# Moving the next batch's convolution on TensorE from the start of a slot to the end of the one before, with VectorE's order kept

## What is computed

```python
h = layernorm(x) * (1 + ca) + sa
xz = h @ in_proj_w.T;  x_, z = split(xz)             # 256 + 256 channels
u  = silu(causal_conv4(x_) + conv_b)                 # depthwise, 4 taps
dt, Bm, Cm = split(u @ x_proj_w.T)                   # 8 + 16 + 16
delta = softplus(dt @ dt_w.T + dt_b)
state_t = state_{t-1} * exp(delta_t * A) + (delta_t * u_t) * B_t   # 256 x 16 states
y_t = sum_n state_t[n] * C_t[n]
x = x + ga * ((y + u * D) * silu(z)) @ out_proj_w.T
h = layernorm(x) * (1 + cb) + sb
x = x + gb * (shared_ffn(h) + top2_of_8_expert_ffn(h))             # exact gelu, 256 hidden
```

## Time and profile before

| | |
|---|---|
| median of 3 runs | 685.6 us (685.33 to 688.16) |
| the profiled execution | 684.8 us |
| its span in the profile | 683.1 us |
| PE busy | 593.3 us (87%) |
| DVE busy | 598.3 us (88%) |
| ACT busy | 489.7 us (72%) |
| POOL busy | 320.2 us (47%) |
| mean granted TensorE clock | 0.955 |

### The profile page before, as it was taken

How to read it: one execution, slowest core, us unless ns; L and a number is a source line. 1 busy time by engine, 2 the same in 40 slices (tenths; PEclk the granted TensorE clock), 3 DMA queues, 4 the chain that set the end, 5 groups by cost and what they waited for, 6 DMA issues and landing times.

```text
span 683.1 us, 9767 instructions
## 1 busy us (share of the span) xinstructions
PE 593.3 (87%) x3646; PEld 466.5 (68%) x3646; DVE 598.3 (88%) x713; ACT 489.7 (72%) x861; POOL 320.2 (47%) x171
## 2 busy tenths in 40 slices
PE   5684478899989998999989998999979947998897
PEld 4243345689657965788567966787668936798686
DVE  5399999999999999999999999999998999798416
ACT  3689535999589976989589957998598925962460
POOL 1036556446654556446653656446543664464000
PEclk9787589999999999999999999999999968999999
DMA  7423333314432235133531343223522442220000
GB/s 221 161 92 140 123 139 142 125 70 169 163 128 82 108 128 184 62 124 124 173 124 63 124 160 138 83 103 124 179 103 70 176 156 83 103 78 16 1 1 16
DMA packets 26705, 77.87 MB, mean 114 GB/s; under 512 B 3025, under 2 KB 17570, under 8 KB 18466
## 3 DMA queue, kind: packets, MB, share of 16 engines
q1 hardware_dynamic: 26178, 76.82, 31.1%
q10 hardware_dynamic: 480, 0.43, 0.2%
HBM read 74.61 MB, written 2.62 MB: 113 GB/s over the span
## 4 chain that ended last, share of the span: by engine, by line
PE 53%; DVE 31%; issue 7%; ACT 5%; POOL 2%; DMA 1%; DVEq 0%; POOLq 0%; ACTq 0%
DVE state L1206 15%; PE psum L677 12%; PE psum L516 10%; DVE psum L1197 8%; PE psum L543 5%; PE psum L645 5%; PE psum L647 4%; PE psum L646 4%; PE psum L687 3%; POOL state L433 2%; PE psum L662 2%; PE psum L565 1%; ACT L866 1%; DVE out_sb L1244 1%; PE psum L799 1%
## 5 line engine op out<-in xcount | busy, mean ns | idle before, releaser
L433 POOL TENSOR_TENSOR state<-state,bc 128x1024 f32<-128x1024 f32 x127 | 300.1, 2363 | 291.8 <-DVE psum L1197 291.8
L1206 DVE TENSOR_TENSOR_SCAN state<-decay,psum 128x1024 f32<-128x1024 f32 x128 | 292.2, 2283 | 21.9 <-PE psum L516 9.5
L885 ACT ACTIVATE decay<-delta,a_neg 128x511 f32<-128x511 f32 x256 | 166.1, 729 | 10.4 <-DVE state L1206 10.3
L516 PE MATMUL psum<-ident,state 128*128 128x128 f32 x1024 | 139.0, 283 | 33.6 <-POOL state L433 33.4
L1197 DVE TENSOR_TENSOR psum<-bc,du 128x1024 f32<-128x1024 f32 x128 | 157.6, 1231 | 4.8 <-DVE state L1206 0.5
L516 PEld LDWEIGHTS psum<-ident,state 128*128 128x128 f32 x1024 | 120.3, 146 | 56.0 <-POOL state L433 44.9
L677 PE MATMUL psum<-down_w,h 128*128 128x128 f32 x896 | 109.9, 276 | 0.0
L677 PEld LDWEIGHTS psum<-down_w,h 128*128 128x128 f32 x896 | 104.4, 192 | 5.3 <-issue 5.3
L1014 ACT ACTIVATE h<-psum,vec 128x512 f32<-128x512 f32 x144 | 97.0, 688 | 2.1 <-PE psum L647 0.6
L980 ACT ACTIVATE gT_mix<-psum,w 128x128 f32<-128x128 f32 x224 | 64.8, 388 | 20.0 <-PE psum L687 14.4
L645 PE MATMUL psum<-h_hi,up_hi 128*128 128x512 f32 x144 | 59.2, 411 | 10.7 <-DVE h_lo L1310 6.7
(11 more groups left out here) (151 smaller groups left out, 638.3 us busy)
## 6 DMA issues: line engine op xcount, KB each, us to landing
bc<-bc_rows SPq DMA_DIRECT2D x64, 1024.0 KB, 4.7
x_sb<-_attn_hidden_states_dram SPq DMA_DIRECT2D x9, 256.0 KB, 2.8
x<-_attn_hidden_states_dram SPq DMA_DIRECT2D x7, 256.0 KB, 3.0
out_dram<-out_sb SPq DMA_DIRECT2D x7, 256.0 KB, 2.4
h<-in_L_ffn_rw_dram SPq DMA_DIRECT2D x1, 1024.0 KB
bc_rows<-rows SPq DMA_DIRECT2D x8, 64.0 KB, 4.8
h<-in_L_wmod_dram ACTq DMA_DIRECT2D x1, 384.0 KB
h<-in_L_attn_in_proj_w_dram SPq DMA_DIRECT2D x1, 256.0 KB, 4.7
```

The costliest lines, as they stand in the source:

```text
L433: pool.tensor_tensor(state[:, u % STATE_RING, :, :], state[:, u % STATE_RING, :, :], bc[:, pair % BC_RING, 1, first:first + NU, :], ALU.mu ...
L516: last = nc.tensor.matmul(Y[q][:, t * P:(t + 1) * P], state[:, u % STATE_RING, s, t * P:(t + 1) * P], ident[:, :], start=False, stop=(u in ...
L885: last = nc.scalar.activation(decay[:, r, s, 1:L], delta[:, b.p, q, 1:L], ACT.Exp, scale=a_neg[:, q, k:k + 1])
L1206: nc.vector.tensor_tensor_scan(state[:, u % STATE_RING, :, :].rearrange("p n t -> p (n t)"), decay[:, u % DECAY_RING, :, :].rearrange("p n ...
```

## The change

PE's queue is rearranged in four places. `conv_in` of the batch after next moves from the start of a slot to the end of the one before: its first half before state sum 12, its second half after it, and both ahead of `acc_transpose`. State sum 12 moves with it to the end of the slot, and `mix_add` of the last expert block stands behind that sum. At the start of the next slot `x_proj` stands between state sums 13 and 14, `z_proj` between 14 and 15. `x_transpose` goes ahead of its step's expert block, and on ACT `h_rows` goes from step 6 to step 3, and `acc_rows` behind the decays of units 3 and 4. The convolution's wait for the banks is for each bank its own. DVE, POOL and SP keep their order.

```diff
@@ conv_in (PE)
-                    if not (isinstance(n.i, int) and n.i < 3):
-                        pe.wait_ge(mixmul_done, DOWNS * (n.i - 2))
-                    elif n.i > 0:
+                    if 0 < n.i < 3:
                         pe.wait_ge(sp_abs, Q * n.i)
+                if n.i >= 3:
+                    pe.wait_ge(mixmul_done, DOWNS * (n.i - 2) - 1 + q)
@@ slots (PE), start
-                if n:
+                if n and not a:
                     conv_in(n, 0)
-                if a:
-                    y_add(a, UN - 4)
-                if n:
                     conv_in(n, 1)
                 if a:
                     y_add(a, UN - 3)
-                    y_add(a, UN - 2)
...
                 if a:
-                    y_add(a, UN - 1)
+                    y_add(a, UN - 2)
                 if n and n.i > 0:
                     z_proj(n, 0)
                     z_proj(n, 1)
+                if a:
+                    y_add(a, UN - 1)
@@ slots (PE), end
                 for u in range(8, UN - 2):
+                    if m and u == 10:
+                        x_transpose(m, n, a)
                     for j in MIX_AT[u]:
                         if a and j + 2 < DOWNS:
                             down(a, j + 2)
-                        if a:
+                        if a and j < DOWNS - 1:
                             mix_add(a, j)
-                    if m and u == 10:
-                        x_transpose(m, n, a)
                     if b and u < UN - 3:
                         y_add(b, u - 1)
+                if b and m:
+                    conv_in(m, 0)
+                if b:
+                    y_add(b, UN - 4)
+                if a:
+                    mix_add(a, DOWNS - 1)
+                if b and m:
+                    conv_in(m, 1)
                 if a:
                     acc_transpose(a)
@@ tail (PE)
-                for u in range(UN - 4, UN - 1):
+                for u in range(UN - 3, UN - 1):
                     y_add(a, u)
@@ slots (ACT)
-                    if m and j == 6 and m.i != 1:
+                    if m and j == 3 and m.i != 1:
                         h_rows(m)
...
                     mix_scaled(a, DOWNS - 1)
+                if n:
+                    decays(n, 3)
+                    decays(n, 4)
+                if a:
                     acc_rows(a)
                 if n:
-                    for u in range(3, AHEAD):
-                        decays(n, u)
+                    decays(n, 5)
```

## The result

| | before | after |
|---|---|---|
| median of 4 runs each | 685.47 us (684.85 to 688.16) | 705.12 us (705.08 to 706.11) |
| the profiled execution | 684.8 us | 706.11 us |
| its span | 683.1 us | 703.1 us |
| mean granted clock | 0.955 | 0.926 |
| period of slots 1 to 5 | 75.06 us | 78.54 us |

The change makes the kernel slower by 19.7 us: the ratio is 1.0282, with a 95% interval of 1.0254 to 1.0311. The forecast was 699.2 us, 694 to 704: the direction is right, the time lies 1.1 us above the range.

The account below looks back on a forecast made before the run. DVE and PE looked equally busy; PE had 4.4 us to spare at `finish`, nothing at `gate_y`. Five slots at 2.8 - 0.2 = 2.6 us (13.0) plus 0.7 make 13.7 on 684.8: 698.5, predicted as 699.2 on the median's scale, range 694 to 704.

Parts of the forecast that it names:

- `finish` 2.8 us late: End of slot, batches 1 to 5: DVE's `finish` waits for the later `acc_transpose`, starting at 254.58 instead of 251.74.
- ScalarE's lag: `h_rows` at step 3 delays scaling of expert blocks 3 to 5, making PE 0.55 us later; bounds 0 and 1.0.
- `gate_y` gives back 0.2: At `gate_y`, sum 15 no longer makes DVE late, so 0.2 us per slot come back, net 2.6.
- Slot 7, 0.7: Last slot: add 7 stands behind sum 12 and ends at 623.44, not 622.77, so 0.7 us go into the tail.
- as worked out: The main case: all terms hold, 699.2 us, chance 0.72, its own range 695.5 to 702.
- Is anything given back in the next slot?: Start of next slot: nothing found; expert matmuls wait for DVE again, and scan 7's 0.53 us wait for sum 3 stays.
- part-given-back rival: At scan 7, a DVE 2.6 us later finds sum 3 done: 11.1 us lost, or 696.7; chance 0.10.
- the clock falls: PE's holes before sum 15 and `g_transpose` lower its clock; `gate_y` waits 0.79 more, five times: 703.2; chance 0.07.
- The rule on weight loads: PE's headroom judged by weight loads, 55.64 of 75 us: 19 us free, so the 7.75 us ahead of `acc_transpose` could fit.

Follow-up runs that it names:

- e2: The changed kernel with `h_rows` back at step 6 of ScalarE; 701.87 us, ratio 1.0206 to the kernel before.
- e3: The changed kernel with idle transposes in PE's holes, ahead of and behind sum 15 and ahead of the expert matmuls; 701.24 us, ratio 1.0203 to before.
- e14: The changed kernel with idle transposes only ahead of `x1_transpose` (21 for 14) and of the expert matmuls (7); 699.72 us, ratio 1.0186 to before.
- e7: The kernel before with eight short idle DVE instructions in slot 0 that shift all that follows; 687.19 us, ratio 0.9995 to before.
- e1: The changed kernel with `finish` moved behind scan 15 in DVE's order; 697.42 us, ratio 1.0151 to the kernel before.
- e13: The changed kernel with idle transposes only ahead of state sum 15 and of `g_transpose` (ten each); 704.22 us, ratio 1.0247 to before.
- e10: The kernel before with more idle transposes only: ahead of `x1_transpose`, ahead of the expert matmuls and in slot 7; 685.38 us, ratio 1.0000 to before.
- e8: The changed kernel with eight short idle DVE instructions in slot 0 that shift all that follows; 706.22 us, ratio 1.0251 to before.
- e4: The changed kernel with `acc_transpose` ahead of the second half of the convolution on PE; 703.86 us, ratio 1.0225 to before.
- e9: The changed kernel with the old slot start, `h_rows` and `acc_rows` places, `finish` behind scan 15 and more idle transposes; 687.71 us, ratio 1.0035 to before.
- e12: e10 with the next convolution's first half ahead of `acc_transpose` and slot 7 rearranged (sums 3 to 5, `finish` of batch 6); 684.88 us, ratio 0.9974 to before.

## Why the prediction was off, step by step

*`finish` 2.8 us late: right.* 2.81 to 2.83 in four slots and 2.47 in slot 3, in the place and behind the instruction named. Its parts: the queue from add 6 to `acc_transpose` 8.62 us (8.63 foreseen), ScalarE's lag 0.69 by e2 (0.55 foreseen, bounds 0 and 1.0). The lag lies ahead of add 6, 29.42 us behind sum 3 for 28.74 before, and not behind it: so `finish` starts 9.25 us after add 6, where the sum gives 254.58 - 244.70 = 9.88.

*`gate_y` gives back 0.2: right,* 0.16 by the two starts of `gate_y` and `finish`. Some 0.1 us a slot in other places eats up most of it; slots 1 to 5 without the part of scan 7 lose 17.42 - 3.81 = 13.6 us, and 13.0 were foreseen.

*Slot 7, 0.7: right at `finish`* (0.69), but scan 7 gave 0.78 back, from its wait of 4.0, as a stretch of before is missing there. That part is luck: nothing in the runs ties it to the change.

*The range* has a slip of its own: the terms given for "as worked out" make 695.8 to 701.5, and not 695.5 to 702. It decides nothing.

*"Is anything given back in the next slot? ... sum 3 behind the expert matmuls, which start at the same place on DVE's clock as before": the step that failed.* They start at the same place, and the part-given-back rival falls with it. But the step took their length as fixed. It grew by 0.74 us, through 3.4 us at half clock, and scan 7 waits 0.76 longer. That makes 3.81 us in slots 1 to 5, 0.76 in slot 6 and 1.40 in the tail, 6.0 of the 6.3 us that the span lies above the sum (683.1 + 13.7 = 696.8 foreseen, 703.1 measured). e3 takes the clock's part out of scan 7 and its period falls from 78.54 to 77.79 us; e14 does it for the experts alone and has the same period, at 699.7 us.

*The rival "the clock falls".* It had the right event, a chance of 0.07, and a price per slot, 0.79, that agrees with the 0.76 measured by luck alone, since it was read from another wait. Two things were wrong in it. Its place: it was priced at `gate_y`, by the row of slot 7. There the first stretch costs nothing, as it begins at 189.7 us, when sum 15 (187.23) and `gate_y` (188.36) have started. The right question was what each later part of PE's work would cost at half clock, and the expert matmuls are where DVE's next wait for PE hangs on 13.55 us of them. The trace of before had that price: 14.33 us in slot 7, and a wait of 4.01 at scan 7. And its "against": "before the change a hole of 1.75 us in each slot left the clock at 1.00". One trace at 1.00 was taken as a bound. e7, the same order set off by half a microsecond, has a stretch in each slot, and in e1 equal slots differ in it. The Trainium skill (TensorE: Matmul & The Clock Gate, What's actually happening) says that TensorE falls to half its clock when it has been idle; the traces agree in kind, but in the slots of after the falls come behind holes of only 0.88 to 1.32 us, and in slot 2 of e7 none ahead is longer than 0.24.

*The rule on weight loads.* By the Trainium skill (Perfetto Trace Analysis, Identifying the Most-Contended Engine) the 58.49 us of weight loads in 78.55 would by estimate leave 20 us free. The 2.83 us wait of `finish` says no: PE's queue is in order, and what counted was the 4.36 us ahead of one instruction.

*What stays open:* what sets off a stretch at half clock in one slot and not in its neighbour. In the changed kernel filling the holes took the stretches right behind them away (e3 but for one, e13, e14). But holes are neither enough (slot 5 of e14) nor needed (e7, and slots 2 of e10 and 3 of e3, where no hole ahead is over 0.24 us), so what the change does to the clock is shown only in so far as the changed kernel has a stretch in the experts of all of slots 1 to 6, in the profiles of after and e8, and the old order in none of them, in those of before and e7.

## What to carry to other kernels

Count an in-order queue's spare time at each instruction that another engine waits for, not per slot: here it was 4.36 us at `finish`, nothing at `gate_y`, and less than nothing at scan 7. Removing one such wait shows the next one that it covered (e1, e4, e9, e12), so cost a reordering at all of them together. And where a change makes new holes in TensorE's queue, price the next long run of matmuls at half clock, even when the slots of before show 1.00, and look for one slot or tail in the trace where it has happened already. Idle transposes right ahead of that run are a cheap test, and here they took its stretch away (e14). They are no free cure: in e10 they used up spare time, and a stretch that cost nothing without them cost about 0.5 us a slot.

## What was not expected of the hardware

The granted clock can fall to 0.50 for about 3.4 us inside a slot in which PE is busy 73.90 of 78.55 us, with no hole of PE longer than 1.32 us, and rise again while PE goes on. In e7 it falls in slot 2 when the longest hole in the 14 us ahead was 0.24 us. The 512-column matmuls of the experts then start 0.43 us apart, not 0.235. The same order of instructions, set off by 0.48 us, had five such stretches or none in slots 1 to 5 (e7 and before), and no cost in time (ratio 0.9995). And equal slots of one execution can differ in it (e1).

What a stretch costs depends on where it falls: 1.40 us in the tail, where the expert matmuls run without a hole; 0.76 in a slot, where a wait of 0.53 us for ScalarE goes away with it; nothing where PE has 1.75 us to spare right behind it (e7).
